# Seven layer norms of a batch applied on ScalarE with a per-row scale and bias instead of on VectorE, with small tiles of their own

## What is computed

```python
def _layernorm(x, axis=-1, eps=1e-05):
    m = jnp.mean(x, axis=axis, keepdims=True)
    v = jnp.var(x, axis=axis, keepdims=True)
    return (x - m) / jnp.sqrt(v + eps)
...
    # inside _L0_attn_ref, ahead of its projections: a norm of its own, then * ln_w + ln_b
...
    x = _layernorm(x + _L0_attn_ref(x, ...))     # a: rope, 16 heads, weights 1 + s + s*s/2
    x = _layernorm(x + _L0_xattn_ref(x, ctx))    # b: masked softmax attention over the context
    x = _layernorm(x + _L0_ffn_ref(x, ...))      # c: 8 experts, the top 2 mixed
    x = _layernorm(x + _L1_attn_ref(x, ...))     # d: delta rule, short and long filters, gates
    x = _layernorm(x + _L1_xattn_ref(x, ctx))    # e: softmax attention over the context
    x = _layernorm(x + _L1_ffn_ref(x, ...))      # f: gated FFN on inputs rounded to FP4
```

## Times and profile before

| | |
|---|---|
| median of 3 runs | 4395.78 us (4394.23 to 4397.1) |
| the profiled execution | 4401.85 us, span from first to last instruction 4399.9 us |
| busy, share of the span | PE 77%, PE weight loads 60%, DVE 60%, ACT 37%, POOL 7% |
| granted PE clock, mean | 0.887 of full speed |
| the applies (L1538) | 224 instructions on DVE, 47.0 + 23.4 + 11.8 us busy |

### The profile page before, as it was taken

One profiled execution on the slowest core, in us unless ns is written; L12 is line 12 of the kernel. 1 busy time (PEld: TensorE's weight loads), 2 busy tenths in 40 slices (PEclk: granted clock), 3 DMA queues, 4 the chain that ended last, 5 costly groups with the idle time before them and its releaser, 6 DMA issues.

```text
span 4399.9 us, 64768 instructions
## 1 busy us (share of the span) xinstructions
PE 3407.8 (77%) x22532; PEld 2643.9 (60%) x22532; DVE 2618.4 (60%) x5927; ACT 1639.0 (37%) x3066; POOL 315.0 (7%) x696
## 2 busy tenths in 40 slices
PE   1687878787887878788787888878788887878854
PEld 0465757566675756567575666657566665756652
DVE  4336484756748475674847557484665738466553
ACT  1333333443333434333334433333433333444311
POOL 1001010100101010010101001010100101010010
PEclk7788989899999989999898899999889899989966
DMA  2020111101111110101111011111001111100100
GB/s 84 1 68 25 63 33 63 32 23 45 30 63 33 63 32 25 44 28 63 32 63 32 16 48 33 63 32 63 18 22 57 33 63 32 51 22 29 52 13 3
DMA packets 183454, 175.67 MB, mean 40 GB/s; under 512 B 58952, under 2 KB 147680, under 8 KB 183136
## 3 DMA queue, kind: packets, MB, share of 16 engines
q1 hardware_dynamic: 183136, 171.27, 12.2%
HBM read 156.55 MB, written 14.68 MB: 39 GB/s over the span
## 4 chain that ended last, share of the span: by engine, by line
PE 49%; DVE 25%; issue 11%; ACT 7%; POOL 5%; DMA 2%; SPq 1%; DVEq 0%; PEldq 0%; PEld 0%; ACTq 0%; POOLq 0%
PE bank L699 27%; DVE region L1790 8%; PE bank L733 6%; PE bank L787 3%; DVE region L1749 2%; ACT pt_f L1194 2%; PE bank L754 2%; PE bank L767 2%; POOL region L679 2%; POOL region L677 2%; DVE nm_f L1571 2%; ACT split_f L1205 1%; PE bank L708 1%; PE bank L1013 1%; DMA gram_scratch<-region 1%
## 5 line engine op out<-in xcount | busy, mean ns | idle before, releaser
L1194 ACT ACTIVATE pt_f<-bank 128x512 f32<-128x512 f32 x768 | 416.0, 595 | 274.8 <-PE bank L767 274.1
L699 PE MATMUL bank<-xTb,c_w 128*128 128x256 f32 x2048 | 498.3, 401 | 0.0
L699 PE MATMUL bank<-c_w,region 128*128 128x256 f32 x2048 | 465.6, 381 | 0.0
L1790 DVE SCALAR_TENSOR_TENSOR region<-vpad,cols,region 128x256 f32<-128x256 f32 x1024 | 451.9, 483 | 16.0
L699 PEld LDWEIGHTS bank<-xTb,c_w 128*128 128x128 f32 x2048 | 408.7, 203 | 69.7 <-issue 10.4
L1723 DVE SCALAR_TENSOR_TENSOR yb<-bank,comb,yb 128x256 f32<-128x256 f32 x256 | 112.1, 479 | 531.3 <-PE bank L699 531.3
L1293 ACT ACTIVATE region<-bank,cols 128x256 f32<-128x256 f32 x512 | 212.8, 470 | 568.2 <-PE bank L699 568.2
L699 PEld LDWEIGHTS bank<-c_w,region 128*128 128x128 f32 x2048 | 384.8, 190 | 51.7 <-issue 0.2
L733 PE MATMUL bank<-identb,split_f 128*102 128x128 bf16 (+1 forms) x4096 | 315.8, 248 | 101.6 <-DVE split_f L1556 81.0
L733 PEld LDWEIGHTS bank<-identb,split_f 128*102 128x102 bf16 (+1 forms) x4096 | 300.2, 149 | 131.6 <-issue 85.4
L767 PE MATMUL bank<-qT_f,kT_f 102*128 102x256 bf16 (+1 forms) x1536 | 281.7, 284 | 121.3 <-ACT pt_f L1194 97.0
(11 more groups left out here) (305 smaller groups left out, 5744.8 us busy)
## 6 DMA issues: line engine op xcount, KB each, us to landing
c_w<-in_c_w SPq DMA_DIRECT2D x256, 512.0 KB, 4.6
gram_scratch<-region SPq DMA_DIRECT2D x16, 512.0 KB, 2.6
x<-in_x SPq DMA_DIRECT2D x16, 256.0 KB, 4.4
ctxf<-in_ctx SPq DMA_DIRECT2D x16, 256.0 KB, 4.6
ctxb<-in_ctx SPq DMA_DIRECT2D x16, 256.0 KB, 6.8
out_dram<-x SPq DMA_DIRECT2D x16, 256.0 KB, 2.2
region<-gram_scratch SPq DMA_DIRECT2D x128, 8.0 KB
inverse_scratch<-region SPq DMA_DIRECT2D x32, 64.0 KB
```

The lines of the kernel that those rows point to most:

```text
L699: mm = pe.matmul(out_ap, l, r, start=(i == 0), stop=(i == len(pairs) - 1))
L1194: act.activation(dst, PS[use].rearrange("p (c s) -> p c s", c=c), func, **kw).then_inc(*PS.drained(use))
L1790: ins = dve.scalar_tensor_tensor(dst[:, c, :], x, w_[:, c, k:k + 1], dst[:, c, :], ALU.mult, ALU.add)
```

## The change

The mean is negated and stored (`nmu`) by one more DVE instruction ahead of `ve`; POOL multiplies it with rstd to `shift_` behind a wait for its own power; ACT then computes Identity(rstd * x + shift_) with two pointer operands per instruction. Every norm gets its own `stats`, `mv`, `ve`, `nmu`, `rstd` and `shift_`. The applies stand in ACT's program in the segments in which they stood in DVE's. DVE keeps a wait where it would overwrite what ACT still reads or read what ACT writes: for x2 in a_apply and x7 in f_apply at the old places, for x6 at the head of f_in as before, and two new ones ahead of writes to `yb` and `yf`.

```diff
-        mv = {g: sb(f"mv_{g}", [P, T, 2]) for g in "fb"}
-        ve = {g: sb(f"ve_{g}", [P, T]) for g in "fb"}
-        rstd = {g: sb(f"rstd_{g}", [P, T]) for g in "fb"}
+        norms = ("a0", "a", "b", "c", "d", "e", "f")
+        mv = {l: sb(f"mv_{l}", [P, T, 2]) for l in norms}
+        ve = {l: sb(f"ve_{l}", [P, T]) for l in norms}
+        nmu = {l: sb(f"nmu_{l}", [P, T]) for l in norms}
+        rstd = {l: sb(f"rstd_{l}", [P, T]) for l in norms}
+        shift_ = {l: sb(f"shift_{l}", [P, T]) for l in norms}
...
             def rsqrt(b, l, g):
+
+                pows[0] = 0
+                pool.sem_clear(s_pow)
 
                 var, r = LN[l]
                 pool.wait_ge(*var(b))
-                pool.tensor_tensor(rstd[g][:, :], ve[g][:, :], neghalf[:, 0:T], ALU.pow).then_inc(*r.up)
+                pool.tensor_tensor(rstd[l][:, :], ve[l][:, :], neghalf[:, 0:T], ALU.pow).then_inc(s_pow, 1)
+                pows[0] += 1
+                pool.wait_ge(s_pow, pows[0])
+                pool.tensor_tensor(shift_[l][:, :], nmu[l][:, :], rstd[l][:, :], ALU.mult).then_inc(*r.up)
...
+            def ln_apply(b, l, src, dst, sig):
+
+                act.wait_ge(*LN[l][1](b))
+                for t in range(T):
+                    ins = act.activation(dst[:, t, :], src[:, t, :], ACT.Identity, bias=shift_[l][:, t:t + 1], scale=rstd[l][:, t:t + 1])
+                ins.then_inc(*sig.up)
...
+                yield "c_apply"
+                ln_apply(b, "c", yb, x4, xo["x4_ready"])
...
+                yield "e_apply"
+                act.wait_ge(*stored(b, 0))
+                ln_apply(b, "e", yf, x6, xo["x6_ready"])
...
+                yield "f_apply"
+                ln_apply(b, "f", yf, x7, xo["x7_ready"])
...
-                dve.tensor_scalar(ve[g][:, :], mv[g][:, :, 1], EPS, None, ALU.add).then_inc(*LN[l][0].up)
-
-            def ln_apply(b, l, g, src, dst, sig):
-                dve.wait_ge(*LN[l][1](b))
-                for t in range(T):
-                    ins = dve.tensor_scalar(dst[:, t, :], src[:, t, :], mv[g][:, t, 0:1], rstd[g][:, t:t + 1], ALU.subtract, ALU.mult)
-                ins.then_inc(*sig.up)
+                dve.tensor_scalar(nmu[l][:, :], mv[l][:, :, 0], -1.0, None, ALU.mult)
+                dve.tensor_scalar(ve[l][:, :], mv[l][:, :, 1], EPS, None, ALU.add).then_inc(*LN[l][0].up)
...
                 yield "a_apply"
-                ln_apply(b, "a", "f", yf, x2, xo["x2_ready"])
+                dve.wait_ge(*xo["x2_ready"](b))
...
                 yield "c_comb"
+                dve.wait_ge(*xo["x5_ready"](b, 0))
                 residual(b, "c_y", yb, x3)
...
+                dve.wait_ge(*xo["x3_ready"](min(b + 2, NB) if isinstance(b, int) else b + 2, 0))
                 link("f", dve.tensor_tensor(yf[:, :, :], a.on, x5[:, :, :], ALU.add))
                 ln_stats(b, "e", "f", yf)
-                yield "e_apply"
-                dve.wait_ge(*stored(b, 0))
-                ln_apply(b, "e", "f", yf, x6, xo["x6_ready"])
...
                 yield "f_apply"
-                ln_apply(b, "f", "f", yf, x7, xo["x7_ready"])
+                dve.wait_ge(*xo["x7_ready"](b))
```

More of the change, by code:

```diff
@@ L321, in decoder @@
         xTb = sb("xTb", [P, C, S])
-        stats = {g: sb(f"stats_{g}", [P, T, 6]) for g in "fb"}
-        mv = {g: sb(f"mv_{g}", [P, T, 2]) for g in "fb"}
-        ve = {g: sb(f"ve_{g}", [P, T]) for g in "fb"}
-        rstd = {g: sb(f"rstd_{g}", [P, T]) for g in "fb"}
+        norms = ("a0", "a", "b", "c", "d", "e", "f")
+        stats = {l: sb(f"stats_{l}", [P, T, 6]) for l in norms}
+        mv = {l: sb(f"mv_{l}", [P, T, 2]) for l in norms}
[3 more added lines that the diff above has]
+        shift_ = {l: sb(f"shift_{l}", [P, T]) for l in norms}
         scrap = {g: sb(f"scrap_{g}", [P, 1]) for g in "fb"}
@@ L412, in decoder @@
         stored = signal("stored", 1, 16)
-        LN = {l: (signal(f"{l}_var", 1), signal(f"{l}_rstd", 1)) for l in ("a0", "a", "b", "c", "d", "e", "f")}
+        LN = {l: (signal(f"{l}_var", 1), signal(f"{l}_rstd", 1)) for l in norms}
         xo = {n: signal(n, 1) for n in ("h_ready", "x2_ready", "x3_ready", "x4_ready", "x5_ready", "x6_ready", "x7_ready")}
@@ L460, in decoder @@
         s_blocks = sem("blocks_step")
+        s_pow = sem("norm_pow")
         primed = sem("primed")
@@ L1229, in _ @@
             a = at_
+            def ln_apply(b, l, src, dst, sig):
[3 more added lines that the diff above has]
+                ins.then_inc(*sig.up)
             def layer_a(b):
                 qs, ks = (a.rest[:, :, H * i:H * i + H, :].rearrange("p t h d -> p t (h d)") for i in range(2))
+                yield "a_norm"
+                ln_apply(b, "a0", x1, hf, xo["h_ready"])
                 yield "a_rope"
@@ L1250, in layer_a @@
                 evac(b, "a_onT", oTf[:, :, :])
+                yield "a_apply"
+                ln_apply(b, "a", yf, x2, xo["x2_ready"])
             def layer_b(b):
@@ L1275, in layer_b @@
                 evac(b, "b_onT", oTf[:, :, :])
+                yield "b_apply"
+                ln_apply(b, "b", yf, x3, xo["x3_ready"])
             def layer_c(b):
@@ L1373, in layer_d @@
                 evac(b, "d_onT", knT[:, :, :], ACT.Identity, scale=col("onorm"))
+                yield "d_apply"
+                ln_apply(b, "d", yb, x5, xo["x5_ready"])
             def layer_e(b):
@@ L1527, in ln_stats @@
                 for t in range(T):
[L1528 removed]
+                    ins = dve.bn_stats(stats[l][:, t, :], src[:, t, :])
                 link(g, ins)
                 for t in range(T):
[L1531 removed]
+                    ins = dve.bn_aggr(mv[l][:, t, :], stats[l][:, t, :])
                 link(g, ins)
[L1533 to L1539 removed]
+                dve.tensor_scalar(nmu[l][:, :], mv[l][:, :, 0], -1.0, None, ALU.mult)
+                dve.tensor_scalar(ve[l][:, :], mv[l][:, :, 1], EPS, None, ALU.add).then_inc(*LN[l][0].up)
             def residual(b, use, y, x):
@@ L1685, in layer_b @@
                 yield "b_apply"
-                ln_apply(b, "b", "f", yf, x3, xo["x3_ready"])
             def layer_c(b):
@@ L1880, in layer_d @@
                 yield "d_apply"
-                ln_apply(b, "d", "b", yb, x5, xo["x5_ready"])
             def layer_e(b):
```

4 lines of the change are left out of this document (1 added, 3 removed).

## The result

Medians: 4621.32 us after (4 runs, 4621.16 to 4625.03), 4395.0 us before (4 runs, 4391.06 to 4397.1). The ratio is 1.0518 with a 95% interval of 1.05 to 1.0536: the change costs 226 us. Forecast were 4603 (4545 to 4665) and slower at 0.96.

The account below looks back on a forecast made before the run. Hand-overs between engines were taken to bound the kernel, no engine being full. Terms of 1.6 + 0.7 + 5.2 + 3.8 + 0.9 + 2.0 = 14.2 us, times 14 = 199, 207 with lighter bodies, gave 4603 us, range 4545 to 4665.

Parts of the forecast that it names:

- Norm c: c's apply stands behind `e_o1`'s evacuation on ACT, so x4's transposes and L812 come later: +1.6 us, bounds 1.4 and 1.75.
- Norm a0: Behind L812, where PE sits idle for the norm, the whole longer chain counts: +0.7 us per body.
- The chain price: Added time per norm from DVE's negation, POOL's multiplication and ACT's slower pair: 0.7 us, between 0.4 and 1.3.
- Norm e: The apply on ACT stands behind layer d's projections, so x6, its quantising and the rope come late: +5.2 us.
- Clock ahead of layer f's second half: PE's idle there grows from 2.84 to 6 us and can bring half clock: 0 to 2.5 us, 1.2 taken.
- Norm f: ACT's weights of layer a begin 5.0 us late behind x7, delaying L812 and DVE's division: +3.8 us, clock 0.8 more.
- Norm b: Between layers PE waits for x3; the chain and norm d's pair ahead of the evacuation add 0.9 us.
- Edges: Bodies with fewer layers: 3.5 us at some five places, about 4.5 for norm e without layers a and b.
- the signs listed: In the profile: x6 wait some 10 us, rope behind, division waiting about 3, PE idle some 6, DVE 60 to 70 lower.
- Only latency: Rival: ACT has room everywhere; only a0, b and x7's wait cost 0.7 us each, total 4429; chance 0.06.
- DVE's relief decides: Rival: less DVE work from the rope to the filters saves 71 us, total 4325; chance 0.03.
- The delays feed on: Rival: further half-clock stretches on PE lengthen layer a's attention, 19 us a body and more, above 4670; chance 0.11.

Follow-up runs that it names:

- both experiments on e: Kernel before with norm e's apply alone moved to ACT: 4496.06 us; kernel after with norm e's apply alone returned to DVE: 4525.98 us.
- e and f alone: Kernel before with one apply moved to ACT at its place after: norm e's 4496.06 us, norm f's 4484.76 us.
- the chain alone: Kernel after with all seven applies back on DVE at their old places, negated mean, POOL multiplication and separate tiles kept: 4438.03 us, ratio 1.006.
- f late on ACT: Kernel before with norm f's apply alone on ACT, behind the first weights of layer a (`a_weigh2`): 4376.05 us, ratio 0.9926.
- separate tiles only: Kernel before with `stats`, `mv`, `ve` and `rstd` per norm, nothing else changed: 4411.39 us, ratio 1.0012.
- f late on DVE: Kernel before with norm f's apply still on DVE but later, in `d_fir1`, and its store in `b_in`: 4372.48 us, ratio 0.9927.
- the four kernels with f late: Norm f's apply later: before, on ACT 4376.05 us, on DVE 4372.48; after, on ACT 4523.21, and with c earlier and e on DVE too 4416.74.
- e back on DVE: Kernel after with norm e's apply alone returned to DVE, its POOL multiplication kept: 4525.98 us, ratio 1.0267.
- f back on DVE: Kernel after with norm f's apply alone returned to DVE, its POOL multiplication kept: 4541.0 us, ratio 1.029.

## Why the prediction held, step by step

The offset of after to before at matching instructions of one body (before from 1041.74 on, after from 1073.61 on) gives what each step cost; from there to the same place of the next body it grew from 256.0 to 270.9 us, by 14.9 for 14.2 forecast. As a mean over the 14 full bodies it grew by 15.4, from 257.5 to 273.0 (the forecast's 254 and 268 were averages that took in the lighter bodies at both ends).

- **Norm c**, forecast 1.6: e's division comes 1.4 later. Right, at the lower of its bounds.
- **Norm a0**, forecast 0.7: 1.1. The chain price of 0.7 was right but for the power's extra 0.38, which the forecast's step had explicitly waved off: "DVE is free earlier and takes norm e's statistics meanwhile, which is of no use". It was not neutral. It slowed POOL.
- **Norm e**, forecast 5.2: the rope comes 3.9 later. The mechanism is as forecast, row by row, and both experiments on e confirm it. Mis-sized was the start, a wait of 7.79 us for x6 instead of some 10: layer d's projections ran in 6.59 us instead of 7.77, as the half-clock stretch behind norm a0 fell on less of them, so `beta` came 1.2 us sooner than c's and a0's delays would put it.
- **Clock ahead of layer f's second half**, forecast 1.2: 0. The step failed that said PE's wait there grows to 6 us: it is 1.32. The half-clock stretch fell on the first half instead (7.52 us for 5.00), behind an idle of 2.81 us, and was hidden behind DVE.
- **Norm f**, forecast 3.8 and 0.8 for the clock: 6.3. ACT's first weight is 5.04 us late, as worked out (5.0). What failed is the next step, that ACT paces the heads and passes on just these 5.0: PE ran 1158 to 1164 at 0.55 of its clock, ACT's pairs came 1.30 us apart instead of 1.08, and L824 is late by 6.6. DVE's slack took its part off, as forecast; the division is late by 5.5 instead of 3.65, and the mask's product behind it (L1815 before) adds 0.8 and not "some tenths".
- **Norm b**, forecast 0.9: 1.5, since the four transposes run at half clock (1.11 us instead of 0.65). Right in kind.
- **Clock elsewhere**, forecast 0: +0.5 ahead of the logits, +1.3 at a half-clock spell at 1235 to 1239, and -1.15 given back in layer c's first products.
- **Edges**, forecast 8: 3.4. The spans of the two traces differ by 219.5 us, of which the 14 full bodies are 216.1. The forecast's 4.5 us for norm e in a body without layers a and b can't all have come.

So the number is better than its parts. Too high were c, e, the clock ahead of layer f's second half and the edges; too low were a0, f, b and the clock elsewhere. In the body shown the first kind makes 2.7 us and the second 3.4, and that they nearly cancel is luck. What is not luck is that the two places that cost most, e and f, are the ones named, for the reason named. Of the signs listed, the row of x6, the rope behind it, the division's wait for L824 and DVE's 65 us came; PE's 6 us of idle ahead of layer f's second half did not.

The Trainium skill (ScalarE: Activation LUTs, "What ACT_TABLE_LOAD costs") was cited with an estimate of 585 ns for one apply and 1.08 us for the pair; the trace agrees, with 586 to 613 ns and 1.08 to 1.10 us. By it the sum would have been 5 x 0.03 = 0.15 us a body higher, no difference in the forecast.

**The rivals.** "Only latency" would be 4429; it leaves out the queue, which e and f alone show to be worth 166 us. That the chain alone measured 4438 does not confirm its price: that kernel keeps the applies on DVE, and its 31 us are mostly the clock. "DVE's relief decides" is refuted by the result, 226 us slower with 65 us less work on DVE, and where a kernel was faster DVE's relief had no part: with f late on ACT (DVE relieved of f) and on DVE (not relieved) the ratio is the same, 0.9926 and 0.9927. "The delays feed on" came about in part: half-clock time grew by some 200 us, 14 a body. At most half of that is work lost, 7 us a body, and most of it was hidden: f and b together exceed their forecast by 2.3.

## What to carry to other kernels

An engine that is busy for 37% is not free at a given place: its queue is in order. An instruction that waits for a late operand stops whatever is ready behind it (norm f), and one whose operand is ready waits for what stands ahead of it (norm e). Before work is moved to it, find what stands ahead of and behind the new place and when its operand comes; with norm f some twelve microseconds further down the queue, the same work on the same engine cost nothing. Count what the freed engine does in that time too, and ask of a gain below 1% whether a stage or only the clock gave it.

## What was not expected of the hardware

**One wait, two lengths of half clock.** The bodies of the kernel before are not alike: after three of 256.0 us come ones of 260.1, 260.6, 259.4, 254.2 and 265.1, counted from gate to gate. The difference lies mostly in one stage, between the mask and the logits (46.96 to 54.20). Stretches of 15 us from 18 us behind the mask on, in the columns of the earlier trace rows; first the kernel before, in a body of 256 us and, in the same execution, in the one of 260.6:

```profile
1156.67:1171.67 15.00, 11.66 (x126) 10.74 (x128) 10.88 (x22) 8.13 (x14) 0.00 (x0) 0.89 0.01 1
...
2440.21:2455.21 15.00, 12.25 (x90) 11.54 (x91) 8.86 (x18) 7.53 (x12) 0.00 (x0) 0.57 0.00 1
```

the kernel with separate tiles only, most of whose bodies take 259.4 us:

```profile
1156.35:1171.35 15.00, 12.25 (x90) 11.53 (x91) 8.86 (x18) 7.53 (x12) 0.00 (x0) 0.56 0.00 1
```

and the kernel with f late on DVE, nearly all of whose bodies take 256.0:

```profile
1149.42:1164.42 15.00, 11.65 (x124) 10.77 (x124) 10.72 (x22) 8.15 (x14) 0.00 (x0) 0.89 0.00 1
```

PE waits for the same thing, as long. Its rows in the two bodies of the kernel before, for the same 32 matmuls:

```profile
1159.42 3.29 PE L733 MATMUL bank<-identb,split_f 128*102 128x128 bf16 x32 [3.05 <-DVE split_f L1556]
```

```profile
2442.96 3.65 PE L733 MATMUL bank<-identb,split_f 128*102 128x128 bf16 x32 [3.04 <-DVE split_f L1556]
```

Yet behind it the granted clock is 1.2 GHz for some 3 us in the one and for most of 15 us in the other, which costs 4.6 us a body (51.6 us ahead of the logits instead of 47.0). From the mask to that wait the two bodies can't be told apart: in each of six stretches of 3 us PE's busy time agrees within 0.05 us, at a granted clock of 1.00. So neither this idle nor the 18 us ahead of it fix what follows; that what PE did further back decides it is a guess that no run here tests. I could not steer it. In the traces of the four kernels with f late the stage is 47.0 to 47.9 us in every body, and so it is with e back on DVE; the chain alone and separate tiles show 51.5 us or so in most bodies, and f back on DVE and after in about half. It can make a kernel's time move by 1% without any wait of the program having changed (before alone went from 4390 to 4431 us in 43 runs), and the 0.7% of f late may be the luck of a rhythm more than the worth of the move. That stays open.

**GpSimd beside VectorE.** The power of 128 x 2 took 0.70 us with DVE idle and 1.08 us with DVE adding two SBUF tiles and taking statistics; only that was changed between the kernels. Not every DVE instruction does it: in the kernel before, norm e's power took 0.69 us beside a scaling out of PSUM (L1608), and norm a's took 0.70 us beside an addition with one operand in PSUM (L1827). Whether it is the addition of two SBUF tiles or the statistics was not tried.
